# Expert choice from unscaled products, gate powers for four pairs at once, and tile tables that start with the first 16 batches

## What is computed

```python
x = x + xattn(layernorm(x), ctx, ctx)          # 16 heads of 8, mask on the 77 keys
x = x + ffn(layernorm(x))

def ffn(x):                                     # E = 8 experts, top 2, F = 512
    proj = x @ Wp.T
    pn, sn = l2norm(proj), l2norm(sim_matrix)
    gate_scores = pn @ sn.T / temperature
    top_v, top_i = top_k(gate_scores, 2)
    gate_probs = softmax(top_v)
    comb = sum(one_hot(top_i, E) * gate_probs[..., None], axis=-2)
    h = gelu(x @ W1[e] + b1[e]); eo = h @ W2[e] + b2[e]
    return sum over e of eo[e] * comb[..., e]
```

## Time and profile before

| | |
|---|---|
| median of 3 runs | 398.8 us (393.33, 398.8, 399.27) |
| profiled execution | 394.04 us, span of its instructions 392.2 us |
| mean granted clock of TensorE | 0.975 of 2.4 GHz |
| TensorE, VectorE, ScalarE, GpSimd busy | 351.1, 307.6, 291.8, 251.7 us |
| attention part, tile part, end | to about 213 us, to about 379 us, to 392 us |

### The profile page before, as it was taken

One profiled execution on the slowest core, in us unless ns is written; L12 is line 12 of the kernel. 1 busy time (PEld: TensorE's weight loads), 2 busy tenths in 40 slices (PEclk: granted clock), 3 DMA queues, 4 the chain that ended last, 5 costly groups with the idle time before them and its releaser, 6 DMA issues.

```text
span 392.2 us, 14080 instructions
## 1 busy us (share of the span) xinstructions
PE 351.1 (90%) x3585; PEld 295.2 (75%) x3586; DVE 307.6 (78%) x1042; ACT 291.8 (74%) x851; POOL 251.7 (64%) x415
## 2 busy tenths in 40 slices
PE   8899999999999999999988997987979999989850
PEld 4467777777777777777766887977869999989850
DVE  6778989999999999999899676664544666565787
ACT  4899999999999999999977564454544666565672
POOL 6532577777777777777664477775766666556560
PEclk9999999999999999999999999898998999999995
DMA  3122203331233101300002222221211222129717
GB/s 89 43 79 77 75 31 98 98 97 37 86 98 99 45 31 45 100 23 24 30 18 54 59 61 66 63 62 56 65 49 60 68 71 75 57 63 272 222 35 214
DMA packets 42601, 29.39 MB, mean 75 GB/s; under 512 B 5459, under 2 KB 39327, under 8 KB 42544
## 3 DMA queue, kind: packets, MB, share of 16 engines
q1 hardware_dynamic: 35792, 18.99, 17.9%
q0 software_dynamic: 4320, 8.53, 6.2%
q10 hardware_dynamic: 2432, 1.18, 1.1%
HBM read 17.53 MB, written 11.62 MB: 74 GB/s over the span
## 4 chain that ended last, share of the span: by engine, by line
PE 74%; DVE 14%; issue 7%; ACT 1%; DVEq 1%; POOL 1%; POOLq 0%; ACTq 0%
PE ps_s L755 18%; PE ps_s L766 16%; PE ps_t L646 11%; PE ps_s L630 6%; PE ps_o L657 5%; PE ps_s L620 4%; DVE mx L1339 3%; PE ps_o L727 2%; PE ps_x L716 2%; PE ps_t L748 2%; PE ps_x L677 2%; PE ps_o L665 2%; DVE gv L1434 1%; PE ps_o L671 1%; DVE cxT L1373 1%
## 5 line engine op out<-in xcount | busy, mean ns | idle before, releaser
L582 POOL DMA_INDIRECT results<-eo,didx x71 | 69.5, 979 | 51.8 <-DVE didx L1686 29.2
L755 PE MATMUL ps_s<-xtT,w1c 128*128 128x128 f32 x568 | 79.2, 284 | 7.9 <-DVE xtT L1705 7.4
L755 PEld LDWEIGHTS ps_s<-xtT,w1c 128*128 128x128 f32 x568 | 71.4, 197 | 11.2 <-DVE xtT L1705 10.0
L766 PE MATMUL ps_s<-w2s,hT 128*128 x568 | 78.9, 284 | 0.4 <-ACT hT L1176 0.4
L457 POOL DMA_INDIRECT lists<-rows,slots x64 | 67.0, 1046 | 18.6 <-issue 15.6
L1074 ACT ACTIVATE pT<-ps_t 77x512 f32<-77x512 f32 x128 | 74.0, 594 | 1.9 <-PE ps_t L646 1.8
L646 PE MATMUL ps_t<-identf,pr 128*77 128x128 f32 x512 | 72.8, 275 | 0.9 <-ACT pT L1074 0.8
L1176 ACT ACTIVATE hT<-h 128x512 f32<-128x512 f32 x71 | 44.6, 629 | 37.2 <-PE ps_s L766 20.9
L766 PEld LDWEIGHTS ps_s<-w2s,hT 128*128 128x128 f32 x568 | 71.4, 197 | 0.8 <-issue 0.6
L1172 ACT ACTIVATE w1c<-w1s 128x512 f32 x71 | 44.7, 630 | 32.5 <-PE ps_s L755 21.2
L1723 DVE TENSOR_TENSOR h<-ps_s,b1T 128x512 f32<-128x512 f32 x71 | 49.0, 690 | 22.0 <-PE ps_s L755 17.8
(11 more groups left out here) (217 smaller groups left out, 610.3 us busy)
## 6 DMA issues: line engine op xcount, KB each, us to landing
xt<-lists SPq DMA_DIRECT2D x71, 66.0 KB
ys<-results SPq DMA_DIRECT2D x15, 256.0 KB, 3.6
xin<-in_x_dram SPq DMA_DIRECT2D x16, 128.0 KB
w1s<-in_L_ffn_W_dram SPq DMA_DIRECT2D x8, 256.0 KB
w2s<-in_L_ffn_W_dram SPq DMA_DIRECT2D x8, 256.0 KB
out_dram<-x SPq DMA_DIRECT2D x5, 256.0 KB
cin<-in_ctx_dram SPq DMA_DIRECT2D x16, 77.0 KB
results<-eo,didx POOLq DMA_INDIRECT x71
```

Source lines behind the costliest of these rows:

```text
L582: nc.gpsimd.indirect_dma_start(results, bass.IndirectOffsetOnAxis(ap=didx[:, r:r + 1], axis=0), eo[:, r, :], None, bounds_check=TOPK * NTO ...
L755: last = nc.tensor.matmul(ps_s[:, r, c * P:(c + 1) * P], w1c[:, r, c * P:(c + 1) * P], xtT[:, r, :], start=True, stop=True)
L766: last = nc.tensor.matmul(ps_s[:, 2 + r, 0:D], hT[:, r, c * P:(c + 1) * P], w2s[:, bass.ds(e + c * D, D)], start=(c == 0), stop=(c == FC - 1))
```

## The change

- gates(J) goes: best and best_places work on the unscaled products dots. The differences are multiplied by rn later, for the first 24 batches and for the last 8 at once (differences, writing dn), and the exponentials read dn.
- gate_power(J) per pair becomes gate_powers(J), for four pairs at once, in GpSimd's steps 5, 9 and 13, and at tile 32 for the last four pairs. n2 and rn get a column for each batch. ScalarE's copy of the products waits for the place search of the pair before (idx_ready), no longer for gv_ready.
- residual_start(J+1) stands behind gate_powers in GpSimd's step, no longer at its head.
- The rows of the first 16 batches are counted too (half_table, in VectorE's step 11), and the first table lists their tiles first. All results of the first 16 batches are then back after 49 tiles (HALF_DONE), those of 24 batches as before after 55.
- SP loads chunks 0 to 3 of the results from tile 58 on and chunks 4 and 5 from tile 64 on. EARLY is 17 for 11: 17 batches are summed between the tiles. ScalarE scales chunk 5 only; the order of chunks is 0, 1, 2, 3, 4, 6, 5, 7.
- In give_back the wait for eo_ready stands last; some memsets that space out the scatters (spread) move by one.

The diff, cut to its core:

```diff
@@ constants
+    HALF = NB // 2
+    HALF_DONE = FULL_TILES + NE
+    POWERS = 4
-    PARTS = 3
+    PARTS = (2, 4)
-    HEADS = (4, 6)
+    HEADS = (5, 6)
-    EARLY = 11
+    EARLY = 17
-        SUMMED = (0, 1, 2, 3, 6, 4, 5, 7)
+        SUMMED = (0, 1, 2, 3, 4, 6, 5, 7)
...
@@ SP
-            late = PART_DONE + FRING + 1
+            late, later = HALF_DONE + FRING + 1, PART_DONE + FRING + 1
             steps(sp, load_tile, early, late - 1, early, late - 1, FRING)
-            all_returned(sp, PART_DONE)
-            for j in range(late, max(N_TILES, late + PART // CH)):
-                if j < N_TILES:
-                    load_tile(j, j)
-                if j < late + PART // CH:
+            all_returned(sp, HALF_DONE)
+            for j in range(late, N_TILES):
+                if j == later:
+                    all_returned(sp, PART_DONE)
+                load_tile(j, j)
+                if j - late < HALF // CH:
                     load_results(sp, j - late)
+                elif 0 <= j - later < (PART - HALF) // CH:
+                    load_results(sp, HALF // CH + j - later)
...
@@ GpSimd
-            def gate_power(J, m):
-                r = m % 2
+            def gate_powers(J):
+                s = slice(2 * (J + 1 - POWERS), 2 * (J + 1))
                 after(pool, E["sq_ready"], J)
-                after(pool, E["rn_ready"], J - 1)
+                after(pool, E["rn_ready"], J // POWERS - 1)
                 settled(pool)
-                nc.gpsimd.tensor_scalar(n2c[:, :], n2[:, r, :], NORM_EPS2, 1.0, ALU.max, ALU.mult).then_inc(E["n2_ready"], 1)
-                after(pool, E["n2_ready"], J)
-                after(pool, E["gv_ready"], J - 2)
-                nc.gpsimd.tensor_tensor(rn[:, r, :], n2c[:, :], neghalf[:, :].to_broadcast([P, 2]), ALU.pow).then_inc(E["rn_ready"], 1)
+                nc.gpsimd.tensor_scalar(n2c[:, :], n2[:, s], NORM_EPS2, 1.0, ALU.max, ALU.mult).then_inc(E["n2_ready"], 1)
+                after(pool, E["n2_ready"], J // POWERS)
+                nc.gpsimd.tensor_tensor(rn[:, s], n2c[:, :], neghalf[:, :].to_broadcast([P, 2 * POWERS]), ALU.pow).then_inc(E["rn_ready"], 1)
...
             def step(J, m):
-                if not (known(J) and J + 1 < 2) and has(J, 1):
-                    residual_start(J + 1, m + 1)
                 if has(J, -2):
                     second_power(J - 2, m - 2)
...
                 if has(J, -3, NP - 1):
                     scatter(J - 3, m - 3, 1, 0)
-                if has(J, -2, NP - 1):
-                    gate_power(J - 2, m - 2)
+                if has(J, -2, NP - 1) and (J - 1) % POWERS == 0:
+                    gate_powers(J - 2)
+                if J + 1 >= 2 and has(J, 1):
+                    residual_start(J + 1, m + 1)
                 if has(J, -3, NP - 1):
                     scatter(J - 3, m - 3, 0, 0)
...
@@ ScalarE
-            act.wait_ge(E["diff_ready"], PART // 2)
-            nc.scalar.activation(expd[:, 0:PART], diff[:, 0:PART], ACT.Exp).then_inc(exp_ready, 1)
+            act.wait_ge(E["dn_ready"], 1)
+            nc.scalar.activation(expd[:, 0:PART], dn[:, 0:PART], ACT.Exp).then_inc(exp_ready, 1)
...
@@ VectorE
-            def gates(J, m):
-
-                r = m % 2
+            def differences(part):
+                s = slice(0, PART) if part == 0 else slice(PART, NB)
+                dve.wait_ge(E["diff_ready"], PART // 2 if part == 0 else NP)
+                dve.wait_ge(E["rn_ready"], (PART if part == 0 else NB) // (2 * POWERS))
+                nc.vector.tensor_tensor(dn[:, s], diff[:, s], rn[:, s], ALU.mult).then_inc(E["dn_ready"], 1)
+
+            def best(J):
                 after(dve, E["dots_ready"], J)
-                after(dve, E["rn_ready"], J)
-                for s in range(2):
-                    last = nc.vector.tensor_scalar(gv[:, s, :], dots[:, s, :], rn[:, r, s:s + 1], MASKED, ALU.mult, ALU.max)
-                last.then_inc(E["gv_ready"], 1)
...
+            def half_table(stage):
+                if stage == 0:
+                    dve.wait_ge(cnt_copied, 1)
+                    written(nc.vector.tensor_scalar(tiles_i[:, 0, 0, :], cnt[:, 0, :], float(P - 1), None, ALU.add))
+                    return
...
             sum_most(15, 15, 0)
+            differences(0)
             ranks(13)
...
```

More of the change, by code:

```diff
@@ L412, in _ @@
             late_results(sp, 0)
-            for c in (EARLY // CH, 3, 6):
+            for c in (4, 6):
                 store(sp, c)
@@ L568, in _ @@
             scatter(13, 13, 1, 1)
-            spread(16 * 2 - 29)
+            spread(3)
             scatter(13, 13, 1, 0)
-            gate_power(14, 14)
+            spread(4)
             scatter(13, 13, 0, 0)
-            spread(16 * 2 - 28)
+            spread(5)
             scatter(13, 13, 0, 1)
@@ L578, in give_back @@
                 after_tile(pool, FE["didx_ready"], j)
+                after(pool, FE["paced"], j - 2, N_TILES - 5)
                 after_tile(pool, FE["eo_ready"], j)
-                after(pool, FE["paced"], j - 2, N_TILES - 5)
                 settled(pool)
@@ L595, in between @@
                     scatter(NP - 2, NP - 2, k // TOPK, k % TOPK)
-                    spread(5 + k)
+                    spread(6 + k)
                 elif j == 6:
-                    gate_power(NP - 1, NP - 1)
                     destinations(NP - 1, NP - 1)
+                elif j == 32:
+                    gate_powers(NP - 1)
                 elif j in (19, 22, 25, 28):
@@ L602, in between @@
                     scatter(NP - 1, NP - 1, k // TOPK, k % TOPK)
-                    spread(9 + k)
-            steps(pool, give_back, 0, N_TILES - 1, LOOPED + 9, N_TILES - 6, FRING, between)
+                    spread(10 + k)
+            steps(pool, give_back, 0, N_TILES - 1, LOOPED + 17, N_TILES - 6, FRING, between)
         @block.tensor
@@ L1084, in gated @@
                 after(act, E["g_done"], J)
-                after(act, E["rn_ready"], J - 2)
                 after(act, E["sq_ready"], J - 1)
@@ L1652, in beside @@
                 elif j == 8:
-                    gates(NP - 1, NP - 1)
                     best(NP - 1)
@@ L1681, in beside @@
                     table_rows(1)
+                elif j == 53:
+                    differences(1)
             def places(j, m):
@@ L1744, in step @@
                     tables(0, 10)
-                if has(J, -3, NP - 1):
-                    gates(J - 3, m - 3)
                 if known(J) and J == PART // 2 + 3 + 1:
@@ L1782, in step @@
                     maximum(J, 0, 0)
-                if known(J - 0) and J - 0 == PART // 2 + 3:
-                    counted()
+                if J in (HALF // 2 + 3, PART // 2 + 3):
+                    counted(0 if J == HALF // 2 + 3 else 1)
                 if has(J, 0):
@@ L1852, in _ @@
             tables(0, 10)
-            gates(13, 13)
             tables(0, 11)
             less_maximum(15, 1, 0)
+            tables(0, 12)
             best(13)
@@ L1882, in _ @@
             tile(-1, -1)
-            gates(14, 14)
             best(14)
@@ L1896, in _ @@
             second_sum(EARLY - 1)
-            first_sum(EARLY)
-            second_sum(EARLY)
-            dve.wait_ge(weighted, 1)
-            wide_sum(3, 0)
-            dve.wait_ge(weighted, 2)
-            wide_sum(3, 1)
+            for b in range(EARLY, 5 * CH):
+                first_sum(b)
+                second_sum(b)
             for stage in range(3):
@@ L1905, in _ @@
             dve.wait_ge(p_step, 6)
-            for c in SUMMED[4:]:
+            for c in SUMMED[5:]:
                 after_y(dve, c)
-                if c == 4:
-                    dve.wait_ge(weighted, 3)
+                if c == 5:
+                    dve.wait_ge(weighted, 1)
                     wide_sum(c, 0)
-                    dve.wait_ge(weighted, 4)
-                    wide_sum(c, 1)
-                elif c == 5:
-                    for b in range(c * CH, (c + 1) * CH):
-                        first_sum(b)
-                    dve.wait_ge(weighted, 5)
+                    dve.wait_ge(weighted, 2)
                     wide_sum(c, 1)
```

142 lines of the change are left out of this document (78 added, 64 removed).

## The result

| | before | after |
|---|---|---|
| median, us | 398.4 (393.3 to 399.3, 4 executions) | 461.8 (460.4 to 463.3, 4 executions) |
| span of the profiled execution, us | 392.2 | 461.5 |
| start of the last kbd | 187.3 | 247.7 |
| start of the first W1 matmul of the tile part | 213.0 | 275.7 |
| start of the last eo | 379.2 | 449.1 |

The account below looks back on a forecast made before the run. TensorE, VectorE and ScalarE, all full in the attention part, were taken as the bound. 394.0 + 34 - 0.8 + 4.4 + 1.2 + 0.6 - 0.5 = 432.9, plus 16.8 for the clock, gave 449 us; range 430 to 463.

Parts of the forecast that it names:

- Part 6: Attention part: TensorE's clock falls to half after each stall, 1.4 us paid twelve times, +16.8 us; 0 without a fall.
- Part 2: Removing VectorE's two gates instructions between maximum and context saves 0.26 us per pair in the attention part.
- Part 1: GpSimd's moved add delays the x load; kbd to maximum takes 5.96 us instead of 2.81, +3.15 us a pair.
- Case D: Attention part: the moved add stays hidden and only savings are left, 391.9 us, no change within 2%; chance 0.05.
- A: Attention part: stall with half clock after it, 449 us, own range 440 to 462; chance 0.6.
- B: Attention part: stall, but TensorE's clock stays up or falls rarely, 433 us; chance 0.25.
- Part 3: GpSimd's powers of four pairs ahead of the add cost 2.2 us before a load, twice, +4.4 us.
- Parts 4 and 5: Added table work on VectorE +1.2 us, exponential waiting for dn +0.6; the end, bound by the last chunk's load, -0.5.
- Part 4: Tables: some seven added small VectorE instructions, +1.2 us, and ScalarE's exponential waiting for dn, +0.6 us.

Follow-up runs that it names:

- the second pair: The kernel before and the changed kernel, both unchanged, timed and profiled again on another chip: 391.0 us and 456.8 us, ratio 1.168.

## Where the prediction was right, and which of its terms failed

The mechanism was right: late add, late load, stall, half clock. The sum was not. It put the change at 55.7 us; the two profiles are 69.3 apart, and the medians 63.4 and, in the second pair, 65.6. That 461.8 still lies in the range owes something to luck: the range has 5 us for a slower execution, and the median of before is itself 4.4 above the 394.0 from which the sum starts. Three terms failed. The tile part, which was to keep its length and so stood at nothing, grew by 7.2 us in the first pair (1.2 in the second). Part 6, the clock, was put at 16.8 and cost 17 to 20. And the saving of Part 2, 0.26 a step, isn't there.

**Part 1, the moved add: right.** Kbd to maximum was forecast at 5.96 us and is 186.87 - 180.95 = 5.92. The landing was put at 2.1 and is 2.2. Kbd can't start earlier: it waits for kT, as before. Twelve steps stall; SP's load comes 3.2 us after kbd. Case D was rightly ruled out by the row of kbd's idle time. Over the twelve loads, though, the time from SP's issue to the first statistics instruction is 2.2 to 3.1 us, 2.4 on the mean: 0.3 a step more than the 2.1 assumed.

**Part 6, the clock: right in kind, too small.** It was forecast at 1.4 a step and is 1.7 between the two kernels with and without the fall, 20.1 us instead of 16.8 (17.1 against the second profile of the changed kernel). The forecast took one fall of 1.7 us of full speed for each of twelve steps, 20.4 in all. There were eleven, three of them twice as long, 23.9 in all, and with TensorE kept busy one of 1.7 was left. So 22.2 us of full speed more were lost and 20.1 us of time; 0.2 us for each fall was covered, as forecast. The choice between A and B hung on three idles of the tile part, and they told true. What the Trainium skill tells in the page "TensorE: Matmul & The Clock Gate", section "HAM oscillation — how this bites in real kernels", of bursts that each begin at half rate holds here in the main: eleven of the twelve stalled bursts have a fall. In seven the queries, the first matmuls behind the wait, ran at half speed throughout (1.2 us for the two, against 0.70 at full clock); in the others the fall began later.

**Part 3, the powers: right, with the clock on top.** The eight columns themselves were forecast well (2.2 with the clamp; 1.67 + 0.28 and a gap, 2.0). With TensorE kept busy, the first of the two steps takes 17.8 us against 15.5, so 2.3; the second, 19.2, has the one fall that is left. In the changed kernel such a step takes 20.1 us where its neighbours take 17.1, so 3.0, and in both the fall is the long one, behind an idle of 5.0 us. In the second profile the step with a short fall takes 18.8, 1.8 more than its neighbours. So a delay ahead of a stalled load is passed on whole, and what comes on top goes with the longer fall of the clock. Taken out of the way, the powers gave back 2.2 and 3.3.

**Part 2, the removed gates: the gain isn't there.** In the version with the add behind second_power most steps take 12.2 to 12.5 us, as before: 0.26 less in each was forecast, and the fourteen steps without half_table are 0.6 us shorter in all. In the chain of the kernel before, the gates stood as one link (gv). In the version with the add behind second_power the chain of a step holds TensorE alone, but for one instruction of ScalarE (start, us, what):

```profile
113.28 1.08 PE ps_o L665 x32
114.36 0.28 PE ps_x L713 x2
114.64 0.88 PE ps_t L654 x8
115.52 0.54 PE ps_o L735 x2
116.06 0.99 PE ps_t L654 x8
117.05 0.45 PE ps_o L673 x4
```

By this chain the 0.26 us saved on VectorE only uncovered TensorE, which has no gap left. That error is worth some 3 us, and it is why the rest of the change was forecast as a gain.

**Parts 4 and 5: about right.** The stretch from the last kbd to the first tile grew by 2.3 us (forecast 1.8), by 1.2 in the version with the add at the head. The 1.4 us of half_table come in the attention part: 2.6 for all of Part 4, where 1.8 were forecast. VectorE's dn holds the exponential for 1.1 us (forecast 1.3). The end is bound by the landing of the last chunk, as said:

```profile
272.66 0.22 ACT L1282 ACTIVATE expd<-dn 128x24 f32<-128x24 f32 x1 [1.11 <-DVE dn L1434]
...
457.04 1.14 DVE L1634 SCALAR_TENSOR_TENSOR x<-ys,p,x 128x128 f32<-128x128 f32 x4 [1.26 <-DMA ys<-results]
```

From the last eo to the end it is 12.4 us instead of 13.0: 0.6 won, 0.5 forecast.

**The sum.** Forecast up to the last kbd: 34 - 0.8 + 4.4 + 16.8 = 54.4; it was 60.4 (58.5 in the second pair). The clock is 3.3 us of the difference. The other 2.7 are in the stalls themselves: with TensorE kept busy the last kbd came 40.3 us later than before, where 37.6 were forecast at full clock. The later landings and the missing saving of Part 2 are each large enough for it, and half_table is there too; the runs don't part them.

The 7.2 us of the tile part were not forecast at all. They are not of the change as far as the runs show. On the two chips on which the kernel before takes 368 us the tile part is 143.0 us long in that kernel (profiled on one of them) and 142.4 to 142.6 in four versions of the changed one. On the other chips VectorE waits in some tiles for 1.2 to 3.7 us, mostly for a matmul's result: 15 times, 27.5 us in all, in the profiled execution of before and 20 times, 40.0 us, in that of after; 16 and 17 times in the second pair; not once in the profile of before on a quick chip. What makes these waits, and whether the changed kernel has more of them in every execution, is open.

## What to carry to other kernels

Before an instruction is moved down an engine's list, follow who waits for its last read: here a 0.7 us add with no urgent result of its own freed a buffer, and whether it could be moved was decided by the 3.3 us of margin of the load behind it. A stall on a full pipeline costs its length, and more if TensorE's clock falls behind it; keeping TensorE busy through the stall tells the two apart in one run. An instruction can also be slowed by what runs beside it: where a move costs time and none of the waits explains it, compare the durations of the same instructions in both traces. When an edit saves time on one of several engines that are all full, ask which of them the chain would go through next, before the saving is counted.

## What the runs showed of the hardware

- A tensor_scalar on VectorE (128x256 f32, two of them in a step) took mostly 0.72 to 0.88 us for the pair in the versions with the add elsewhere, and 2.89 us where GpSimd ran an add and kbd behind each other without a gap. It ended 0.16 us behind them.
- Pow on GpSimd took 0.56 us for one column, 0.72 for two, 1.67 for eight: 0.16 for each further column. Four pairs at once cost 1.95 us with their clamp, one by one 4 x 0.97.
- Twelve idles of 1.9 to 5.0 us in TensorE (39.4 us in all) brought the mean clock of 32 us to 0.84 to 0.94; thirteen idles of 1.0 to 2.6 us (add right behind kbd, 23.4 us in all) left it at 0.95 to 1.00.
- Behind idles of 2.3 to 3.2 us the half clock cost 1.7 us of full speed, behind those of 5.0, 5.0 and 3.9 us 3.4. This is not strict: in the second profile of the changed kernel 3.4 us went behind idles of 3.1 and 4.9, and 1.7 behind one of 5.0. 28 matmuls with no use in each of the twelve stalls left one fall of eleven.
- The same kernel took 366.4 us on one chip and 389.2 on another (spans), with the last kbd at 184.7 and 186.2. So 21 of the 23 us lie behind the attention part, where on the second chip VectorE and ScalarE wait in some tiles for 1.2 to 3.9 us, mostly for a matmul's result. In neither are all four engines idle at once for more than 0.4 us. No run here was made to find the cause.
